# Order of the products inside one place of an attention and expert kernel: long products of both tiles first, then the diagonal blocks of both

## The chip, the cores and the metric

The kernel runs on one core of one Trainium2 chip. The metric is the device time of one execution in microseconds (us), the median over several runs. In the profile PE is TensorE with its matmuls, PEld are TensorE's weight loads (a matmul is a load of its stationary operand and the product itself), DVE is VectorE, ACT is ScalarE, POOL is GpSimd, and SP and ACT issue DMAs. L661 is line 661 of the kernel.

## The reference, cut to what matters

Sixteen sequences of 512 tokens with 256 channels pass through one transformer layer: attention with 16 heads of 16 channels, rotary positions and an ALiBi bias, a layer norm, a mixture of 8 experts with the best 2 chosen (and a shared expert), and a second layer norm.

```python
q = q * cos + _rotate_half(q) * sin
k = k * cos + _rotate_half(k) * sin
attn = jnp.einsum('bhqd,bhkd->bhqk', q, k) * SCALE
diff = jnp.where(pos[None, :] - pos[:, None] > 0, 0.0, pos[None, :] - pos[:, None])
attn = attn + (diff[None, :, :] * slopes[:, None, None] * MAX_BIAS)[None]
w = jax.nn.softmax(attn, axis=-1)
out = jnp.einsum('bhqk,bhkd->bhqd', w, v)
...
x = _layernorm(x + attention(x))
x = _layernorm(x + silu(x @ sW1 + sb1) @ sW2 + sb2 + two experts of eight, weighted)
```

## The kernel before, in words

All work is cut into numbered places s. A place from 0 to 511 (NC is 512) computes one 256 by 512 piece of the scores of one head, as two tiles k = 0 and 1 of 128 queries by 512 keys. It does this twice, for two purposes, with 14 places (LAG) between them:

- The score part of place s (tile pS, two banks, one for each k) gives the scores with queries on the partitions. DVE takes the negated maximum of every row (`row_max`, L965), one `tensor_reduce` for each k. The maxima go back through DRAM into two rows of the query operand.
- The turned part of place d = s - 14 (tile pT, two banks) gives the transposed scores, with the maxima subtracted. ACT takes their exponentials (`exps`, L1417), one activation for each k, into ee.

Each bank gets one long product (`score_rows` L661, `turned_rows` L682; 512 columns, 62 or 64 rows of the array) and on top of it two short diagonal blocks of 64 columns in bf16 (`score_block` L667, `turned_block` L688), which carry the part of the bias inside the diagonal. The second block of a bank raises s_s or s_t, and DVE or ACT starts on that bank. Score part and turned part of one place use opposite halves of the array's rows (slice 64 * hh), so their products can run side by side.

pS and pT have one bank for each k and no second set. So the long product of tile k of place s waits until the reduction of tile k of place s - 1 has ended (s_max), and the turned one until the exponential of tile k of place d - 1 has (s_exp).

The function `pair(s)` writes out the order on TensorE. APART holds all 32 residues, so in every place the order is: long products of k = 0 (score, turned), blocks of k = 0, long products of k = 1, blocks of k = 1. In the first 14 places, which have no turned part, and the last 14, which have no score part, `beside` (L696) puts a product on the unused bank, whose result nobody reads.

Behind `pair(s)` TensorE has in the same place whatever falls due by tables of fixed offsets: the products of the exponentials with the values (`weighted_values`, L710), the projections of queries, keys and values (L734, L743), the output projection (L756), and the transposes and expert products (L829, L837, L845, L847). DVE and ACT go through the same places with their own parts of these jobs, each queue in program order; `row_max(s)` and `exps(s - LAG)` come first in their place.

Of the kernel before, what the change touches and what calls it, by code (L numbers as in the profile page):

```python
# [6 lines left out]
ALU = mybir.AluOpType  # L7
ACT = mybir.ActivationFunctionType
# [3 lines left out]
F32R = mybir.dt.float32r  # L12
U32 = mybir.dt.uint32
AX = mybir.AxisListType.X
# [4 lines left out]
NC = NB * 32  # L19
LAG = 14  # L20


APART = tuple(range(32))
PV = (1, 3)
EPS = 1e-5
NBOUND = 7
# [173 lines left out]
def _build(nc, ctx, A, out):  # L200
    def sb(name, shape, dt=F32):
        return ctx.enter_context(nc.sbuf_tensor(name, shape, dt))

    def ps(name, shape, dt=F32):
        return ctx.enter_context(nc.psum_tensor(name, shape, dt))
# [4 lines left out]
    def sem(name):  # L210
        return ctx.enter_context(nc.semaphore(name))
# [4 lines left out]
    qa = [sb(f"qa{i}", [128, 2, T]) for i in range(4)]  # L216
    ka = [sb(f"ka{i}", [128, 2, T]) for i in range(4)]
    ee = sb("ee", [128, 2, 7, T])
# [24 lines left out]
    tri = sb("tri", [128, 4, 128], BF16)  # L243
    mAB = sb("mAB", [128, 2, 8, 64], BF16)
    sl = sb("sl", [128, H])
    slb = sb("slb", [128, H], BF16)
    slp = sb("slp", [128, 7, H])
    slc = sb("slc", [128, 1])
    negm = sb("negm", [128, 2, 4, 4])
# [53 lines left out]
    pS = ps("pS", [128, 2, T])  # L303
    pT = ps("pT", [128, 2, T])
# [53 lines left out]
    s_s, s_max, s_t, s_exp, s_pv, s_ev = (sem(n) for n in ("s_s", "s_max", "s_t", "s_exp", "s_pv", "s_ev"))  # L358
# [279 lines left out]
    def _(e):  # L638
# [6 lines left out]
        def score_wait(s):  # L645
            if s == 0:
                warm(WARM[3])
                e.wait_ge(p_w, 16)
                warm(WARM[4])
            g = s // 8  # L650
            e.wait_ge(qk_in[g % 4], group_in(g))
            if s == 0:
                e.wait_ge(l_tri, 32)
                e.wait_ge(s_slope, 4)

        def score_rows(s, k):
            if s > 0:
                e.wait_ge(s_max, 2 * (s - 1) + k + 1)
            g, i, t, hh = s // 8, (s // 4) % 2, 2 * (s % 2) + k, (s // 2) % 2
            r = slice(64 * hh, 64 * hh + 62)  # L660
            e.matmul(pS[:, k, :], qa[g % 4][r, i, t * 128:t * 128 + 128].bitcast(F32R),  # L661
                     ka[g % 4][r, i, :].bitcast(F32R), start=True, stop=False)

        def score_block(s, k, a):
            i, t, hh = (s // 4) % 8, 2 * (s % 2) + k, (s // 2) % 2
            r, c0 = slice(64 * hh, 64 * hh + 64), t * 128 + 64 * a
            last = e.matmul(pS[:, k, c0:c0 + 64], tri[r, a, :], mAB[r, 1, i, :], start=False, stop=(a == 1))  # L667
            if a == 1:
                last.then_inc(s_s, 1)

        def turned_wait(d):
            g = d // 8
            e.wait_ge(m_in[g % 2], 32 * (g // 2 + 1))

        def turned_rows(d, k):
            if d > 0:
                e.wait_ge(s_exp, 2 * (d - 1) + k + 1)
            g, kt, i, hh = d // 8, 2 * (d // 4 % 2) + k, d % 2, d // 2 % 2  # L680
            r = slice(64 * hh, 64 * hh + 64)
            e.matmul(pT[:, k, :], ka[g % 4][r, i, kt * 128:kt * 128 + 128].bitcast(F32R),  # L682
                     qa[g % 4][r, i, :].bitcast(F32R), start=True, stop=False)

        def turned_block(d, k, a):
            kt, i, hh = 2 * (d // 4 % 2) + k, 2 * (d // 8 % 4) + d % 2, d // 2 % 2
            r, c0 = slice(64 * hh, 64 * hh + 64), kt * 128 + 64 * a
            last = e.matmul(pT[:, k, c0:c0 + 64], tri[r, 2 + a, :], mAB[r, 0, i, :], start=False, stop=(a == 1))  # L688
            if a == 1:
                last.then_inc(s_t, 1)  # L690

        def beside(p, s, k):

            g, i, t, hh = s // 8, (s // 4) % 2, 2 * (s % 2) + k, (s // 2) % 2
            r = slice(64 * hh, 64 * hh + 62)
            e.matmul(p[:, k, :], qa[g % 4][r, i, t * 128:t * 128 + 128].bitcast(F32R),  # L696
                     ka[g % 4][r, i, :].bitcast(F32R), start=True, stop=True)
# [178 lines left out]
        def pair(s):  # L876
            d = s - LAG
            if 0 <= s < NC:
                score_wait(s)
            if 0 <= d < NC:  # L880
                turned_wait(d)
            apart = s % 32 in APART
            for k in range(2):
                if 0 <= s < NC:
                    score_rows(s, k)
                if 0 <= d < NC:
                    turned_rows(d, k)
                if 0 <= s < LAG:
                    beside(pT, s ^ 2, k)
                if NC <= s < NC + LAG:  # L890
                    if s == NC:
                        e.wait_ge(s_max, 2 * NC)
                    beside(pS, (d & -4) + (0, 2)[d // 2 % 2 == 0], k)
                for kk in ((k,) if apart else (0, 1) if k == 1 else ()):
                    for a in range(2):
                        if 0 <= s < NC:
                            score_block(s, kk, a)
                        if 0 <= d < NC:
                            turned_block(d, kk, a)

        e.wait_ge(s_zb0, 1)
        warm(WARM[0])
        for s in range(FIRST, LAST):
            pair(s)
            for k in range(2):
                w, r = divmod(s - LAG - PV[k], 4)
# [41 lines left out]
    def _(e):  # L948
# [10 lines left out]

        def row_max(s):  # L960
            g, j, t = s // 8, (s // 2) % 4, 2 * (s % 2)
            if s % 32 in APART:
                for k in range(2):
                    e.wait_ge(s_s, 2 * s + k + 1)
                    e.tensor_reduce(negm[:, g % 2, j, t + k:t + k + 1], pS[:, k, :], AX, ALU.max, negate=True).then_inc(s_max, 1)  # L965
            else:
                e.wait_ge(s_s, 2 * s + 2)
                e.tensor_reduce(negm[:, g % 2, j, t:t + 2], pS[:, :, :], AX, ALU.max, negate=True).then_inc(s_max, 2)

        def m_split(g):  # L970
            i = g % 2
# [311 lines left out]
        for x in (*rb2, sb2):  # L1283
            last = e.tensor_copy(x[:, :].bitcast(F32R), zb[:, 0:C])
# [46 lines left out]
        for s in range(FIRST, LAST):  # L1331
            if 0 <= s < NC:
                row_max(s)
# [72 lines left out]
    def _(e):  # L1406
        def exps(d):
            w, j = d // 4, 2 * (d % 2) + d // 2 % 2
            if d > 6:
                e.wait_ge(s_pv, (d - 7) // 4 + 1)  # L1410
            if d == 0:
                e.wait_ge(b_w, 64)
            h = (d // 8 % 4) * 4 + j
            if (d + LAG) % 32 in APART:
                for k in range(2):
                    e.wait_ge(s_t, 2 * d + k + 1)
                    e.activation(ee[:, k, d % 7, :], pT[:, k, :], ACT.Exp, scale=slp[:, 6, h:h + 1]).then_inc(s_exp, 1)  # L1417
            else:
                e.wait_ge(s_t, 2 * d + 2)
                e.activation(ee[:, :, d % 7, :], pT[:, :, :], ACT.Exp, scale=slp[:, 6, h:h + 1]).then_inc(s_exp, 2)  # L1420

        def evacuate(g):
            e.wait_ge(s_pv, 2 * g + 2)
# [114 lines left out]
        for s in range(FIRST, LAST):  # L1538
            if 0 <= s - LAG < NC:
                exps(s - LAG)  # L1540
# [248 lines left out]
```

## Time and profile before

| | |
|---|---|
| three runs | 1585.77, 1590.22, 1663.03 us; median 1590.22 us |
| the profiled execution | 1581.27 us, of which the span from first to last instruction is 1579.5 us |
| mean granted clock of TensorE in it | 0.967 |
| busy: PE, DVE, ACT, POOL | 1443.7, 1143.5, 1022.9, 717.3 us |
| chain that ended last, by engine | PE 65%, DVE 16%, issue 5%, DMA 4%, ACT 3% |

Busy time of an engine is the time covered by its instructions. The ends of matmuls are modelled and they are pipelined, so the distance between the starts of successive instructions tells more than their lengths. A row of the timeline gives start, length, engine, line, operation and the count of merged instructions; the part in brackets is the idle time before it on its engine and what ended it. DVE and ACT instructions in a merged row of two overlap a little.

### The profile page before, as it was taken

The page shows a single profiled execution, that of the slowest core. Times are in us where ns is not written, and L with a number is a line of the kernel's source. Part 1 is how long each engine was busy: PE and PEld are TensorE (multiplying, and loading weights), DVE is VectorE, ACT ScalarE, POOL GpSimd, SP SyncE. Part 2 cuts the span into 40 slices and gives each one's busy share as a digit, 9 for nine tenths or more (in the row PEclk, how much of TensorE's full clock was granted, in tenths as well). Part 3 has the DMA queues.
Part 4 walks back from the last instruction along what each step waited for, and adds up shares of the span by engine and source line. Part 5 has one row for each costly group of instructions (what it writes and reads, how often), then busy time and mean ns, then how long its engine had stood idle before and what let it go on. Part 6 is the DMA issues. An engine that isn't in the chain of part 4 may idle for free.

```text
span 1579.5 us, 33115 instructions
## 1 busy us (share of the span) xinstructions
PE 1443.7 (91%) x11166; PEld 790.4 (50%) x11166; DVE 1143.5 (72%) x2632; ACT 1022.9 (65%) x1742; POOL 717.3 (45%) x654
## 2 busy tenths in 40 slices
PE   7888999999999989999999999999998898888877
PEld 4433444444444445555555544455555555545545
DVE  7675877787787897667666788778875577644677
ACT  1365766676767667767777767676675576666434
POOL 2333363635546453643535353636475443354451
PEclk8799999999999999999999999999999999989899
DMA  7436343334343334555545443445576576368552
GB/s 203 137 95 190 102 123 111 117 111 127 121 124 119 115 109 154 160 162 174 173 154 173 129 144 110 131 159 169 182 226 216 158 221 215 112 209 262 194 155 84
DMA packets 176389, 242.00 MB, mean 153 GB/s; under 512 B 58023, under 2 KB 94974, under 8 KB 176222
## 3 DMA queue, kind: packets, MB, share of 16 engines
q1 hardware_dynamic: 145786, 181.18, 37.7%
q0 software_dynamic: 10752, 29.37, 5.7%
q10 hardware_dynamic: 19684, 29.33, 5.3%
q8 instruction: 91, 1.49, 0.4%
q14 instruction: 76, 0.62, 0.1%
HBM read 152.53 MB, written 91.44 MB: 154 GB/s over the span
## 4 chain that ended last, share of the span: by engine, by line
PE 65%; DVE 16%; SPq 5%; issue 5%; DMA 4%; ACT 3%; another core or an unknown queue 2%; POOL 0%; ACTq 0%; DVEq 0%; POOLq 0%
PE pS L661 18%; PE pV L710 12%; PE pG L734 7%; DVE negm L965 5%; PE pG L756 3%; PE pS L667 3%; PE pG L743 3%; PE pG L837 3%; PE pG L845 3%; PE pT L688 2%; PE pT L682 2%; PE pG L829 2%; PE pG L818 2%; ACT ee L1417 1%
## 5 line engine op out<-in xcount | busy, mean ns | idle before, releaser
L965 DVE TENSOR_REDUCE negm<-pS 128x1 f32<-128x512 f32 x1024 | 658.9, 683 | 281.6 <-PE pS L667 236.8
L1417 ACT ACTIVATE ee<-pT,slp 128x512 f32<-128x512 f32 x1024 | 650.7, 684 | 236.2 <-PE pT L688 208.7
L661 PE MATMUL pS<-ka,qa 62*128 62x512 f32 x1024 | 471.1, 495 | 59.2 <-DVE negm L965 47.9
L682 PE MATMUL pT<-qa,ka 64*128 64x512 f32 x1024 | 471.6, 494 | 8.7 <-ACT ee L1417 7.0
L661 PEld LDWEIGHTS pS<-ka,qa 62*128 62x128 f32 x1024 | 193.0, 188 | 316.8 <-issue 290.8
L710 PE MATMUL pV<-ee,vv 128*32 128x512 f32 (+1 forms) x2048 | 284.1, 627 | 0.0
L667 PE MATMUL pS<-mAB,tri 64*128 64x64 bf16 x2048 | 239.2, 198 | 0.0
L688 PE MATMUL pT<-mAB,tri 64*128 64x64 bf16 x2048 | 236.8, 196 | 0.0
L1604 POOL TENSOR_TENSOR raw<-raw,rope 128x512 f32<-128x512 f32 x61 | 77.9, 1276 | 302.6 <-DVE sh L1005 300.5
L682 PEld LDWEIGHTS pT<-qa,ka 64*128 64x128 f32 x1024 | 191.8, 187 | 20.5 <-issue 11.6
L667 PEld LDWEIGHTS pS<-mAB,tri 64*128 64x128 bf16 x2048 | 117.1, 97 | 132.8 <-issue 101.2
L1624 POOL TENSOR_TENSOR rs<-ve,minus 128x4 f32<-128x4 f32 x32 | 34.2, 1068 | 280.9 <-DVE ve L1053 280.7
L734 PE MATMUL pG<-xT,wqkv 128*128 128x512 f32 x256 | 144.6, 649 | 5.3 <-DVE wqkv L1320 2.9
L1639 POOL DMA_INDIRECT d_x<-x,pos x112 | 113.2, 1010 | 56.6 <-DVE pos L1100 32.3
L688 PEld LDWEIGHTS pT<-mAB,tri 64*128 64x128 bf16 x2048 | 115.9, 96 | 25.5 <-issue 21.2
L1668 POOL TENSOR_TENSOR pvs<-pvs 128x512 f32<-128x512 f32 x31 | 39.4, 1272 | 132.4 <-DVE pvs L990 132.3
L837 PE MATMUL pG<-xgT,wb 128*128 128x256 f32 x308 | 85.5, 402 | 13.9 <-ACT xgT L1505 6.3
L845 PE MATMUL pG<-wb,zbb 128*128 128x256 f32 x308 | 93.4, 396 | 2.1 <-ACT xgT L1505 1.4
L1661 POOL DMA_INDIRECT gg<-d_y,posy x72 | 71.1, 987 | 33.7 <-issue 20.8
L1521 ACT ACTIVATE yb<-pG 128x512 f32<-128x512 f32 x77 | 45.9, 597 | 61.7 <-PE pG L847 47.9
L1616 POOL TENSOR_TENSOR parts<-raw,parts 128x512 fp32r<-128x512 f32 x61 | 77.8, 1275 | 5.0
L1609 POOL TENSOR_TENSOR raw<-raw,sh 128x512 f32<-128x512 f32 x61 | 77.9, 1277 | 4.8
(203 smaller groups left out, 2179.8 us busy)
## 6 DMA issues: line engine op xcount, KB each, us to landing
d_part<-parts SPq DMA_DIRECT2D x63, 512.0 KB, 2.8
qa<-d_part SPq DMA_DIRECT2D x378, 64.0 KB
wb<-in_wb SPq DMA_DIRECT2D x77, 256.5 KB
xg<-d_x SPq DMA_DIRECT2D x77, 256.0 KB
d_y<-yb ACTq DMA_DIRECT2D x77, 256.0 KB
ka<-d_part SPq DMA_DIRECT2D x128, 128.0 KB
xT<-in_xT SPq DMA_DIRECT2D x16, 512.0 KB
ka<-d_part SPq DMA_DIRECT2D x128, 64.0 KB
```

The lines of the kernel that those rows point to most:

```text
L661: e.matmul(pS[:, k, :], qa[g % 4][r, i, t * 128:t * 128 + 128].bitcast(F32R), ka[g % 4][r, i, :].bitcast(F32R), start=True, stop=False)
L667: last = e.matmul(pS[:, k, c0:c0 + 64], tri[r, a, :], mAB[r, 1, i, :], start=False, stop=(a == 1))
L682: e.matmul(pT[:, k, :], ka[g % 4][r, i, kt * 128:kt * 128 + 128].bitcast(F32R), qa[g % 4][r, i, :].bitcast(F32R), start=True, stop=False)
L688: last = e.matmul(pT[:, k, c0:c0 + 64], tri[r, 2 + a, :], mAB[r, 0, i, :], start=False, stop=(a == 1))
L710: last = e.matmul(pV[32 * hh:32 * hh + m, :], vv[b % 2][:, 17 * kt + r0:17 * kt + r0 + m, h], ee[:, k, (4 * w + 2 * (hh % 2) + hh // 2) % ...
L734: last = e.matmul(pG[bk("qk", i, b)][:, :], wqkv[:, c, col:col + 128], xT[b % 2][:, c, :], start=(c == 0), stop=(c == 1))
L837: last = e.matmul(p[:, 0:ROWS], wb[q % 4][:, c * 128:c * 128 + 128], xgT[q % 2][:, c, :], start=(c == 0), stop=(c == 1))
L845: e.matmul(p[:, k * C:(k + 1) * C], zbb[q % 2][:, k * 128:k * 128 + 128], wb[q % 4][:, 256:512], start=True, stop=False)
L965: e.tensor_reduce(negm[:, g % 2, j, t + k:t + k + 1], pS[:, k, :], AX, ALU.max, negate=True).then_inc(s_max, 1)
L1417: e.activation(ee[:, k, d % 7, :], pT[:, k, :], ACT.Exp, scale=slp[:, 6, h:h + 1]).then_inc(s_exp, 1)
L1604: e.tensor_tensor(raw[:, :], raw[:, :], rope[:, 0, :], ALU.mult).then_inc(s_rope, 1)
L1639: e.indirect_dma_start(d_x[g % 2], bass.IndirectOffsetOnAxis(pos[:, b % 2, n, t:t + 1], 0), x1[b % 2][:, t, :], None).then_inc(rows_w, 16)
```

## The change

Inside `pair(s)` the four groups are reordered: long products of k = 0, long products of k = 1, then the blocks of k = 0, then the blocks of k = 1. The waits are split off from the long products (`score_free`, `turned_free`), so that both waits of a k stand ahead of both long products of that k; `beside` now stands ahead of the long products of its k. The semaphores are the same: the second block of each bank raises s_s or s_t, and DVE and ACT still work bank by bank. The branches for places not in APART, which no place took, are gone.

```diff
+        def score_free(s, k):
             if s > 0:
                 e.wait_ge(s_max, 2 * (s - 1) + k + 1)
+
+        def score_rows(s, k):
             g, i, t, hh = s // 8, (s // 4) % 2, 2 * (s % 2) + k, (s // 2) % 2
...
+        def turned_free(d, k):
             if d > 0:
                 e.wait_ge(s_exp, 2 * (d - 1) + k + 1)
...
-            apart = s % 32 in APART
+            def blocks(k):
+                for a in range(2):
+                    if 0 <= s < NC:
+                        score_block(s, k, a)
+                    if 0 <= d < NC:
+                        turned_block(d, k, a)
+
             for k in range(2):
                 if 0 <= s < NC:
-                    score_rows(s, k)
+                    score_free(s, k)
                 if 0 <= d < NC:
-                    turned_rows(d, k)
+                    turned_free(d, k)
                 if 0 <= s < LAG:
                     beside(pT, s ^ 2, k)
...
-                for kk in ((k,) if apart else (0, 1) if k == 1 else ()):
-                    for a in range(2):
-                        if 0 <= s < NC:
-                            score_block(s, kk, a)
-                        if 0 <= d < NC:
-                            turned_block(d, kk, a)
+                if 0 <= s < NC:
+                    score_rows(s, k)
+                if 0 <= d < NC:
+                    turned_rows(d, k)
+            for k in range(2):
+                blocks(k)
```

The matmuls of the long products and blocks also get `skip_group_check=True`, which adds no instruction.

## Rows read from the trace of the kernel before

**Rows 1.** The page, part 1: busy time, share of the span, instructions.
```profile
PE 1443.7 (91%) x11166; PEld 790.4 (50%) x11166; DVE 1143.5 (72%) x2632; ACT 1022.9 (65%) x1742; POOL 717.3 (45%) x654
```

**Rows 2.** Busy time by stretch of time, 200 to 1200 us in five stretches.
```profile
core 0: us, PE busy (x) PEld busy (x) DVE busy (x) ACT busy (x) POOL busy (x), PEclk, DMA share, GB/s
...
sum 1000.00, PE 952.54 PEld 499.81 DVE 759.47 ACT 702.52 POOL 493.85; mean PE 190.51 PEld 99.96 DVE 151.89 ACT 140.50 POOL 98.77
```

**Rows 3.** Costliest groups: busy us, mean ns of one | idle before, releaser.
```profile
L965 DVE TENSOR_REDUCE negm<-pS 128x1 f32<-128x512 f32 x1024 | 658.9, 683 | 281.6 <-PE pS L667 236.8
...
L661 PE MATMUL pS<-ka,qa 62*128 62x512 f32 x1024 | 471.1, 495 | 59.2 <-DVE negm L965 47.9
```

**Rows 4.** Waits of PE: us in total, times, longest.
```profile
PE pS L661 <- DVE negm L965: 47.9, 66, 3.0
...
PE pT L682 <- ACT ee L1417: 7.0, 14, 1.2
```

**Rows 5.** Timeline of PEld, one place without a wait on DVE or ACT.
```profile
706.53 0.18 PEld L661 LDWEIGHTS pS<-ka,qa 62*128 62x128 f32 x1 [0.17 <-issue]
...
706.88 0.10 PEld L667 LDWEIGHTS pS<-mAB,tri 64*128 64x128 bf16 x1 [0.16 <-issue]
...
706.93 0.19 PEld L661 LDWEIGHTS pS<-ka,qa 62*128 62x128 f32 x1
...
707.27 0.09 PEld L667 LDWEIGHTS pS<-mAB,tri 64*128 64x128 bf16 x1 [0.16 <-issue]
...
707.44 0.30 PEld L734 LDWEIGHTS pG<-xT,wqkv 128*128 128x128 f32 x2
```

**Rows 6.** Timeline of DVE and ACT, the same place.
```profile
707.15 1.29 DVE L965 TENSOR_REDUCE negm<-pS 128x1 f32<-128x512 f32 x2 [2.13 <-PE pS L667]
707.25 1.26 ACT L1417 ACTIVATE ee<-pT,slp 128x512 f32<-128x512 f32 x2
```

**Rows 7.** Timeline of PEld and PE, a place of the first 14.
```profile
50.71 0.18 PEld L661 LDWEIGHTS pS<-ka,qa 62*128 62x128 f32 x1 [0.76 <-issue]
50.71 0.29 PEld L696 LDWEIGHTS pT<-ka,qa 62*128 62x128 f32 x2
...
50.71 0.50 PE L696 MATMUL pT<-ka,qa 62*128 62x512 f32 x1
...
51.05 0.39 PE L696 MATMUL pT<-ka,qa 62*128 62x512 f32 x1
```

**Rows 8.** Timeline of DVE and PEld, a place that waits on DVE.
```profile
107.09 1.29 DVE L965 TENSOR_REDUCE negm<-pS 128x1 f32<-128x512 f32 x2 [0.17 <-PE pS L667]
108.30 0.24 DVE L986 RECIPROCAL scr<-sc 128x16 f32<-128x16 f32 x1
108.52 1.29 DVE L965 TENSOR_REDUCE negm<-pS 128x1 f32<-128x512 f32 x2
...
108.43 0.18 PEld L661 LDWEIGHTS pS<-ka,qa 62*128 62x128 f32 x1
```

**Rows 9.** Timeline of ACT and PEld, a short place and its successor.
```profile
1099.09 1.26 ACT L1417 ACTIVATE ee<-pT,slp 128x512 f32<-128x512 f32 x2 [0.68 <-PE pT L688]
...
1098.38 0.18 PEld L661 LDWEIGHTS pS<-ka,qa 62*128 62x128 f32 x1 [0.76 <-issue]
...
1100.28 0.18 PEld L661 LDWEIGHTS pS<-ka,qa 62*128 62x128 f32 x1 [0.83 <-issue]
...
1100.67 0.19 PEld L661 LDWEIGHTS pS<-ka,qa 62*128 62x128 f32 x1
```

**Rows 10.** Timeline of PEld: ends of the two counted sets of intervals.
```profile
30.39 0.18 PEld L661 LDWEIGHTS pS<-ka,qa 62*128 62x128 f32 x1
...
52.65 0.18 PEld L661 LDWEIGHTS pS<-ka,qa 62*128 62x128 f32 x1 [0.33 <-issue]
...
1358.00 0.18 PEld L661 LDWEIGHTS pS<-ka,qa 62*128 62x128 f32 x1 [0.17 <-issue]
...
1376.51 0.18 PEld L661 LDWEIGHTS pS<-ka,qa 62*128 62x128 f32 x1
```

More of the change, by code:

```diff
@@ L20 @@
 LAG = 14
-APART = tuple(range(32))
 PV = (1, 3)
@@ L654, in score_wait @@
                 e.wait_ge(s_slope, 4)
-        def score_rows(s, k):
+        def score_free(s, k):
             if s > 0:
                 e.wait_ge(s_max, 2 * (s - 1) + k + 1)
+        def score_rows(s, k):
             g, i, t, hh = s // 8, (s // 4) % 2, 2 * (s % 2) + k, (s // 2) % 2
@@ L661, in score_rows @@
             e.matmul(pS[:, k, :], qa[g % 4][r, i, t * 128:t * 128 + 128].bitcast(F32R),
-                     ka[g % 4][r, i, :].bitcast(F32R), start=True, stop=False)
+                     ka[g % 4][r, i, :].bitcast(F32R), start=True, stop=False, skip_group_check=True)
         def score_block(s, k, a):
@@ L666, in score_block @@
             r, c0 = slice(64 * hh, 64 * hh + 64), t * 128 + 64 * a
-            last = e.matmul(pS[:, k, c0:c0 + 64], tri[r, a, :], mAB[r, 1, i, :], start=False, stop=(a == 1))
+            last = e.matmul(pS[:, k, c0:c0 + 64], tri[r, a, :], mAB[r, 1, i, :], start=False, stop=(a == 1), skip_group_check=True)
             if a == 1:
@@ L675, in turned_wait, with turned_rows @@
             e.wait_ge(m_in[g % 2], 32 * (g // 2 + 1))
-        def turned_rows(d, k):
+        def turned_free(d, k):
             if d > 0:
                 e.wait_ge(s_exp, 2 * (d - 1) + k + 1)
+        def turned_rows(d, k):
             g, kt, i, hh = d // 8, 2 * (d // 4 % 2) + k, d % 2, d // 2 % 2
@@ L682, in turned_rows @@
             e.matmul(pT[:, k, :], ka[g % 4][r, i, kt * 128:kt * 128 + 128].bitcast(F32R),
-                     qa[g % 4][r, i, :].bitcast(F32R), start=True, stop=False)
+                     qa[g % 4][r, i, :].bitcast(F32R), start=True, stop=False, skip_group_check=True)
         def turned_block(d, k, a):
@@ L687, in turned_block @@
             r, c0 = slice(64 * hh, 64 * hh + 64), kt * 128 + 64 * a
-            last = e.matmul(pT[:, k, c0:c0 + 64], tri[r, 2 + a, :], mAB[r, 0, i, :], start=False, stop=(a == 1))
+            last = e.matmul(pT[:, k, c0:c0 + 64], tri[r, 2 + a, :], mAB[r, 0, i, :], start=False, stop=(a == 1), skip_group_check=True)
             if a == 1:
@@ L961, in row_max @@
             g, j, t = s // 8, (s // 2) % 4, 2 * (s % 2)
[L962 to L968, printed above, removed]
+            for k in range(2):
+                e.wait_ge(s_s, 2 * s + k + 1)
+                e.tensor_reduce(negm[:, g % 2, j, t + k:t + k + 1], pS[:, k, :], AX, ALU.max, negate=True).then_inc(s_max, 1)
         def m_split(g):
@@ L1413, in exps @@
             h = (d // 8 % 4) * 4 + j
[L1414 to L1420, printed above, removed]
+            for k in range(2):
+                e.wait_ge(s_t, 2 * d + k + 1)
+                e.activation(ee[:, k, d % 7, :], pT[:, k, :], ACT.Exp, scale=slp[:, 6, h:h + 1]).then_inc(s_exp, 1)
         def evacuate(g):
```

## The prediction

> **What bounds the kernel now.** I read the page's busy times first: PE is busy 91% of the span, DVE 72%, ACT 65% [rows 1]. Then the stretches: in the middle 1000 us PE is busy 95%, DVE 76%, ACT 70% [rows 2]. So PE sets the pace as a mean, but not by much: DVE and ACT have 1.3 us of work on the two banks in every place and other work besides. Then the groups: of DVE's idle time before the reductions, 237 of 282 us ends with a block of PE [rows 3]; DVE mostly waits for PE, and the other way round PE waits before L661 for DVE 66 times, 47.9 us in all, and for ACT before L682 7.0 us [rows 4]. The reader is to see two loops there: PE through a place, and the hand-over of a bank from PE to DVE or ACT and back. The change shortens the first and lengthens the second, so both must be measured.
>
> I went to the timeline for that. A place without a wait [rows 5] runs: long loads of k = 0 at 706.53, block loads at 706.88 (0.35 later), long loads of k = 1 at 706.93 (0.05 later), blocks at 707.27, next job at 707.44 (0.12 behind the last block). `pair` holds TensorE for 0.90 us. DVE starts at 707.15, 0.61 us behind the place's first load; ACT at 707.25, 0.71 behind it [rows 6]. The two reductions end 1.29 us after they start, so at 1.90 behind the first load.
>
> **Part 1: the order on TensorE.** Nothing is added or removed in number; 8 blocks, 4 long products remain. What is new is that a long load of k = 1 follows a long product of k = 0 in the same half of the array. Two cases in the trace tell what a load does there. A bf16 block load behind a long product starts only 0.34 to 0.35 us behind that product's load, so after the product has streamed [rows 5]. A 32-bit long load behind a 32-bit long product starts under it: in the first 14 places the half used by `beside` has no blocks between its two products, and the two L696 loads together take 0.29 us where one takes 0.18; the second starts 0.11 us behind the first, and its product starts at 51.05, 0.34 behind the first [rows 7]. So in the new order: long loads of k = 0 at 0, of k = 1 at 0.11, second long products at 0.34, block loads at 0.34 + 0.22 = 0.56 (they came 0.22 to 0.23 behind the start of a long product's streaming before: 0.35 less the 0.11 of the load), then the four blocks of k = 0 in 0.05, those of k = 1 in 0.06, and 0.12 to the next job: 0.79 us, or 0.78 with the unrounded starts. Against 0.90 that saves 0.11 to 0.12 us a place where PE runs without waiting. I take 0.12; from below the bound is 0 (no load is hidden), from above 0.18, one whole long load.
>
> The Trainium skill has a rule that speaks against this: "TensorE: Matmul & The Clock Gate", section "Part 3: Packing small matmuls", says that a weight load overlaps a running product only when it goes to another group of rows. By it the saving would be 0, and the case becomes rival C below. The trace disagrees in rows 7, where both L696 loads go to the same rows.
>
> Two waits now stand ahead of one load, where each load had one; one of them becomes an instruction of its own. The nearest rows are a load that waited: it came 0.05 behind the end of the reduction that it waited for, everything of the hand-back included [rows 8]. Where the semaphores are already up, this runs ahead of the array under the products queued there, and costs nothing; a second 0.05 in every place, 26 us, is its bound from above. I take 0, since in most places they are up. That the score's product waits also for the exponential, in the same place where the turned one waited, moves it by a few hundredths of a us. `beside` ahead of its product touches 28 places and costs nothing.
>
> **Part 2: the hand-over of the banks.** The blocks of k = 0 are now queued behind the long products of k = 1, and these behind the waits for the last reduction and last exponential of the place before. Without a wait DVE starts at 0.56 + 0.27 = 0.83 behind the place's first load instead of 0.61 (0.27 is 707.15 less 706.88), so all reductions and exponentials end 0.21 later than now. And the long load of k = 1 wants to start at 0.11 instead of 0.39, that is 0.28 earlier. So the margin between the end of the last reduction (or exponential) and the long load of k = 1 of the next place shrinks by 0.49; 0.12 of this costs nothing, because the load may come that much late under the running product. A place whose margin now is m therefore loses 0.37 - m where m is below 0.37.
>
> In a stretch where DVE never rests, this is seen at its worst [rows 8]: reductions end at 108.38, the long load of k = 1 comes 0.05 later, and DVE finds bank 0 ready and starts again at 108.52. In the new order the blocks of bank 0 stand behind that load, and DVE starts at 108.43 + 0.61 = 109.04, 0.5 us later. The least interval of a place becomes 0.59 + 0.68 + 0.05 + 0.71 = 2.03 us by way of ACT (start to start of its two exponentials, the second, the hand-back, the hand-over); now intervals of 1.42 us occur. A typical short place [rows 9]: loads at 1098.38 and 1100.28, 1.90 apart, exponentials end at 1100.35, the long load of k = 1 is at 1100.67: m = 0.32, so it loses 0.05.
>
> **The sum.** I took all 511 intervals between the first long loads of successive places. In 356 of them PE waits for nothing (the second begins at 52.65, the last ends at 1358.00): 356 x 0.12 = 43 us gained. In 241 (the first is the one whose k = 1 load stands at 30.39, the last at 1376.51) the margin is below 0.37, and the shortages add up to 52 us [rows 10]. The median margin is 0.42. The two add up to +9 us. I counted it in a second way, by length: 157 intervals are shorter than 2.0 (134 with a mean of 1.93, 23 with a mean of 1.52) and grow to 2.02: 134 x 0.09 + 23 x 0.50 = +24 us; 55 between 2.0 and 2.15 shrink by 0.06: -3; of 299 longer ones 201 have no wait and shrink by 0.12: -24; 23 of these 201 have margins below 0.37, +10. That gives +7. I take +8 us. Other work of DVE and ACT between two places is cover for the longer hand-over; if it were gone the 299 longer intervals would still be longer than 2.03, so they need none.
>
> The profiled execution took 1581.3 us, of which 1579.5 are the span; it would become 1589. The median of the runs lies 8.9 us above the profiled execution, so on the median's scale the forecast is 1590 + 8 = 1598 us, +0.5%. A measurement of this kernel tells about 2%, 32 us, from no change.
>
> **The rivals.**
>
> A (slower): the hand-over becomes the pace. The place is the long load of k = 1, which waits for the last exponential of the place before. It decides if the margins count in full: nothing of the lost 0.49 is hidden, because the late load also puts the block loads late. The 293 intervals below 0.49 fall short by 84 us; less the 43 gained that is +41: 1631 us. For it: the median margin of 0.42 is below 0.49, and DVE, busy 76% in the middle [rows 2], has little left to catch up with. Against it: rows 7 show the slack of 0.12 under the product.
>
> B (faster): the shortages are absorbed and the waiting places gain too. 29 of the 52 us of shortage lie in intervals where PE waits already for something, often a DMA; if these cost nothing, 23 remain, and if the 155 waiting intervals gain 0.12 as well (19 us), the sum is -43 - 19 + 23 = -39: 1551 us. For it: many of the shortest intervals catch up behind a longer one. Against it: most waits of L661 are for DVE itself [rows 4], which gets later.
>
> C (slower): the second long load isn't hidden. The blocks of k = 0 come at 0.34 + 0.34 = 0.68, `pair` stays at 0.91, reductions end 0.34 later and the load of k = 1 wants to come 0.05 earlier: shortages below 0.39 add up to 57 us, and no gain: 1647 us. For it: block loads are never seen under a long product. Against it: rows 7.
>
> **How the numbers follow.** Forecast 0.66, A 0.15, B 0.09, C 0.05; 0.05 for anything else, on both sides. The range goes from half of B's gain, -20 (gain 43, shortages only 23 outside waiting intervals), to A's +41: 1570 to 1632. The forecast's own range is 1580 to 1618. Faster by over 2% (below 1558) needs B, 0.07. Slower by over 2% (above 1622) is A, C and a little of the rest: 0.20. Within 2%: 0.73.
>
> **What would show it right or wrong.** In a place without a wait the second L661 load stands 0.11 behind the first, block loads at 0.56, the next job at 0.79; if the second load is at 0.34, it is C. The first reduction starts 0.83 behind the place's first load. Intervals below 1.95 are gone. Waits of PE before L661 for DVE, and before L682 for ACT, grow from 48 and 7 us together to over 80. PE's busy time falls by some tens of us, while the idle time grows by a little more. It is wrong if the intervals above 2.15 don't shrink, or if the short ones don't grow.

## The result and the profile after

The changed kernel takes 1634.6 us (median of four runs, 1627.4 to 1644.9) against 1588.0 for the kernel before on the same chip: ratio 1.0319, with an interval of 1.0279 to 1.0359. It is 3.2% slower. One slow run of the kernel before, 1663.0 us, stands in its median and not in the ratio, which is why the ratio isn't quite the quotient of the two medians. The forecast was 1598, 8 us above the kernel before, with a range from 1570 to 1632. The sign was right; the change cost 47 us by the medians, and the measured time lies 3 us above the range. On a second chip, where the kernel before takes 1545 us, the ratio was 1.0176 (1.0140 to 1.0212).

The page of the changed kernel, parts 1 and 4, answers to [rows 1]:

```profile
PE 1461.0 (89%) x11166; PEld 780.6 (48%) x11166; DVE 1144.6 (70%) x2632; ACT 1016.5 (62%) x1742; POOL 719.7 (44%) x654
...
PE 62%; DVE 11%; SPq 7%; ACT 7%; issue 5%; DMA 5%; another core or an unknown queue 3%; POOL 1%; ACTq 0%; POOLq 0%; DVEq 0%
```

DVE and ACT do the same work in the same time, in a span that is 60 us longer. PE's busy time rose by 17 us, with the same instructions. Its groups, from part 5, answer to [rows 3]:

```profile
L971 DVE TENSOR_REDUCE negm<-pS 128x1 f32<-128x512 f32 x1024 | 658.5, 684 | 353.9 <-PE pS L668 304.0
...
L1419 ACT ACTIVATE ee<-pT,slp 128x512 f32<-128x512 f32 x1024 | 649.6, 684 | 344.9 <-PE pT L689 306.6
...
L662 PE MATMUL pS<-ka,qa 62*128 62x512 f32 x1024 | 444.8, 479 | 92.4 <-ACT ee L1419 41.2
```

A reduction is as long as it was (684 against 683 ns), but DVE waits 304 us for block products, where it waited 237. PE's idle time before the score's long product went from 59 to 92 us, and the largest part of it, 41 us, now ends with an exponential. These two numbers show only a part of the delay, because the modelled ends of the products reach into the time in which TensorE waits. PEld shows more of it, in the idle time ahead of the score's long loads; before and after:

```profile
L661 PEld LDWEIGHTS pS<-ka,qa 62*128 62x128 f32 x1024 | 193.0, 188 | 316.8 <-issue 290.8
```

```profile
L662 PEld LDWEIGHTS pS<-ka,qa 62*128 62x128 f32 x1024 | 179.0, 191 | 421.3 <-issue 329.8
```

It is 104 us more. Part of this has only moved: ahead of the score's block loads (L667, now L668) the idle time fell from 133 to 96 us. The waits of PE, against [rows 4]:

```profile
PE pS L662 <- ACT ee L1419: 41.2, 62, 2.3
PE pS L662 <- DVE negm L971: 24.5, 24, 2.4
```

Before, ACT held PE for 7.0 us and DVE for 47.9. The sum went from 55 to 66 us, and the releaser changed: for the larger part it is ACT now.

A place in which nothing holds TensorE, weight loads alone, against [rows 5]:

```profile
734.43 0.18 PEld L662 LDWEIGHTS pS<-ka,qa 62*128 62x128 f32 x1 [0.23 <-issue]
...
734.54 0.19 PEld L662 LDWEIGHTS pS<-ka,qa 62*128 62x128 f32 x1
...
735.00 0.09 PEld L668 LDWEIGHTS pS<-mAB,tri 64*128 64x128 bf16 x1 [0.28 <-issue]
...
735.23 0.22 PEld L711 LDWEIGHTS pV<-ee,vv 128*32 128x32 f32 x8
```

The second long load comes 0.11 us behind the first, the blocks 0.57, the next job 0.80 (0.91 before). DVE's row of the same place, against [rows 6], starts 0.85 behind the first load (0.62 before):

```profile
735.28 1.29 DVE L971 TENSOR_REDUCE negm<-pS 128x1 f32<-128x512 f32 x2 [1.20 <-PE pS L668]
```

That is the place as it was forecast. But most places don't look like this. Two that follow each other, first the weight loads, against [rows 8]:

```profile
469.94 0.18 PEld L662 LDWEIGHTS pS<-ka,qa 62*128 62x128 f32 x1 [0.83 <-issue]
...
470.45 0.18 PEld L662 LDWEIGHTS pS<-ka,qa 62*128 62x128 f32 x1 [0.32 <-DVE negm L971]
...
470.78 0.11 PEld L668 LDWEIGHTS pS<-mAB,tri 64*128 64x128 bf16 x2
...
472.09 0.18 PEld L662 LDWEIGHTS pS<-ka,qa 62*128 62x128 f32 x1 [0.76 <-issue]
...
472.54 0.18 PEld L662 LDWEIGHTS pS<-ka,qa 62*128 62x128 f32 x1 [0.26 <-DVE negm L971]
```

and ACT's two pairs of exponentials in them:

```profile
469.06 1.27 ACT L1419 ACTIVATE ee<-pT,slp 128x512 f32<-128x512 f32 x2
471.16 1.26 ACT L1419 ACTIVATE ee<-pT,slp 128x512 f32<-128x512 f32 x2 [0.83 <-PE pT L689]
```

The second long load stands 0.51 and 0.45 behind the first, not 0.11. The row names DVE as its releaser, but the pair of exponentials ended last, at 469.06 + 1.27 = 470.33, and the load follows 0.12 behind. The next exponential starts 0.71 behind that load. So from one pair of exponentials to the next it is 471.16 - 469.06 = 2.10 us, of which ACT stands idle for 0.83. Of 497 places with both parts and such a place before them, the score's load of k = 1 follows within 0.12 us behind an exponential in 245, and behind a reduction in 57. In the kernel before, where each load had its own wait, the turned load followed an exponential in 87 places and the score's load a reduction in 92.

### The profile page after: what moved, and what is told of

The parts are those of the page before. It is cut to its first block, busy times and chain, and to the rows that moved or that the text cites. A ratio compares the mean times of both kernels' runs of the same rounds, so it can differ in the third digit from the quotient of the medians.

```text
span 1639.2 us, 34110 instructions
## 1 busy us (share of the span) xinstructions
PE 1461.0 (89%) x11166; PEld 780.6 (48%) x11166; DVE 1144.6 (70%) x2632; ACT 1016.5 (62%) x1742; POOL 719.7 (44%) x654
## 4 chain that ended last, share of the span: by engine, by line
PE 62%; DVE 11%; SPq 7%; ACT 7%; issue 5%; DMA 5%; another core or an unknown queue 3%; POOL 1%; ACTq 0%; POOLq 0%; DVEq 0%
PE pS L662 19%; PE pV L711 12%; PE pG L735 6%; ACT ee L1419 4%; PE pG L744 3%; DVE negm L971 3%; PE pG L757 3%; PE pG L838 2%; PE pS L668 2%; PE pT L689 2%; PE pG L846 2%; PE pG L819 2%; PE pG L806 1%; PE pG L830 1%
## 5 line engine op out<-in xcount | busy, mean ns | idle before, releaser
L662 PE MATMUL pS<-ka,qa 62*128 62x512 f32 x1024 | 444.8, 479 | 92.4 <-ACT ee L1419 41.2
L683 PE MATMUL pT<-qa,ka 64*128 64x512 f32 x1024 | 451.5, 486 | 0.0
L662 PEld LDWEIGHTS pS<-ka,qa 62*128 62x128 f32 x1024 | 179.0, 191 | 421.3 <-issue 329.8
L711 PE MATMUL pV<-ee,vv 128*32 128x512 f32 (+1 forms) x2048 | 295.6, 651 | 0.0
L683 PEld LDWEIGHTS pT<-qa,ka 64*128 64x128 f32 x1024 | 177.6, 190 | 0.0
L668 PE MATMUL pS<-mAB,tri 64*128 64x64 bf16 x2048 | 152.8, 196 | 0.0
L689 PE MATMUL pT<-mAB,tri 64*128 64x64 bf16 x2048 | 151.2, 195 | 0.0
L668 PEld LDWEIGHTS pS<-mAB,tri 64*128 64x128 bf16 x2048 | 90.9, 98 | 95.7 <-issue 64.7
L689 PEld LDWEIGHTS pT<-mAB,tri 64*128 64x128 bf16 x2048 | 89.6, 97 | 11.4 <-issue 11.0
L1605 POOL TENSOR_TENSOR sh<-sh,rope 128x512 f32<-128x512 f32 x61 | 78.1, 1281 | 0.0
```

The costliest lines, as they stand in the source:

```text
L711: last = e.matmul(pV[32 * hh:32 * hh + m, :], vv[b % 2][:, 17 * kt + r0:17 * kt + r0 + m, h], ee[:, k, (4 * w + 2 * (hh % 2) + hh // 2) % ...
```

## The experiments

In the diffs, `free(k)` stands for both waits of a k, `rows(k)` for its long products, `blocks(k)` for its four blocks. Every ratio is to the kernel before on the same chip. Five chips took part; the kernel before takes 1588, 1602, 1544, 1545 and 1545 us on them, so times are compared on one chip, or as ratios.

**e1: the old order with all four waits at the head of the place.** The products are those of before, and only the waits move.

```diff
-for k in range(2): free(k); rows(k); blocks(k)
+for k in range(2): free(k)
+for k in range(2): rows(k); blocks(k)
```

> The order of the products is that of the kernel before; only the waits move: all four of a place (reduction and exponential, k = 0 and 1) stand ahead of its first long product. Theory 1 (hand-over: tile 0 of a place can't be handed on until the last reduction and exponential of the place before have ended, while TensorE itself gets faster by 0.1 us a place): the same long loop as in the changed kernel, about 2.1 us at least for a place, without TensorE's gain. So slower than the changed kernel's 1635 us, by up to 0.1 x 250 = 25 us: 1635 to 1660 us, and no interval of a place below 2.0 us. Theory 2 (the extra wait instruction costs 0.06 us where it is on the path, little else): about 0.06 x 250 = 15 us over before, 1605 us. Theory 3 (the products' new order itself is slow on TensorE, or lowers its clock): no change from before, 1590 us.

Measured: 1708.4 against 1601.7, ratio 1.0676 (1.0629 to 1.0723). The waits of PE:

```profile
PE pS L662 <- ACT ee L1425: 81.3, 108, 7.5
PE pS L662 <- DVE negm L977: 47.6, 47, 2.8
```

Apart from the first two places, which have no turned part, no interval is below 2.11 us; before, a quarter was below 1.96. A late first long load alone, with no product moved, costs 107 us. So the hand-over of the banks is a pace that this kernel runs close to, and more of the waiting ends with ACT. The cost is more than was expected: 6.8%, where 1635 to 1660 us would have been 3% to 4.5% over the kernel before, and twice what the changed kernel loses. TensorE also stood at the lower of its two clock levels for 210 us in this trace (105 in the kernel before, on the first chip), so the 107 us are not the hand-over's pace alone.

**e2: the changed order, with each wait at its own long product again.**

```diff
 for k in range(2):
-    free(k); rows(k)
+    score_free(s, k); score_rows(s, k)
+    turned_free(d, k); turned_rows(d, k)
```

> The changed kernel's order of products, but each wait back ahead of its own product (the score's product waits for the reduction only, the turned one for the exponential only, and no load has two waits ahead of it). Theory 1 (hand-over): nearly the changed kernel, 1620 to 1630 us; the load of the turned product comes 0.05 us behind the exponential instead of 0.11, in about half of the places, so 10 to 15 us of the 47 go. Theory 2 (extra wait): most of it goes, 1600 us or less. Theory 3 (order on TensorE): no change from 1635 us.

Measured: 1633.8 against 1601.7, ratio 1.0224 (1.0174 to 1.0274). ACT's row and the weight loads of one place:

```profile
423.24 1.27 ACT L1417 ACTIVATE ee<-pT,slp 128x512 f32<-128x512 f32 x2 [1.27 <-PE pT L689]
```

```profile
424.49 0.18 PEld L662 LDWEIGHTS pS<-ka,qa 62*128 62x128 f32 x1 [0.32 <-DVE negm L969]
424.56 0.18 PEld L683 LDWEIGHTS pT<-qa,ka 64*128 64x128 f32 x1
```

The exponentials end at 424.51, and the turned load follows 0.05 behind; the score's load no longer waits for them. In the changed kernel it was 0.12 at 470.45, since the wait for ACT there is an instruction of its own (34110 instructions against 33115). Over all places of this kind it is 0.05 here and 0.11 there. What this is worth in time lies between the changed kernel's 1.018 and 1.032, both of other chips, and can't be told from them; most of the loss stays without it.

**e8: the old order, with both waits of a k ahead of its long products.**

```diff
 for k in range(2):
-    score_free(s, k); score_rows(s, k)
-    turned_free(d, k); turned_rows(d, k)
+    free(k); rows(k)
     blocks(k)
```

> The old order of products, but both waits of a tile (reduction and exponential) ahead of both its long products, as the changed kernel has them; this is the price of the extra wait instruction alone. About 100 places are held by the exponential in the trace of before, 0.06 us each: 6 us slower by theory 1, within 10 us. By theory 2 (the extra wait carries the loss) 30 us or more slower.

Measured: 1549.0 against 1543.8, ratio 1.0033 (1.0008 to 1.0057): 5 us, as expected. In the old order, where ACT seldom holds the load, the extra wait costs a third of a per cent.

**e3 and e4: the old order and the changed one, with reductions and exponentials over half of the columns.** Both leave out the other half of the row maxima and of the exponentials, and the products with the values read the first half twice. Product counts and shapes on TensorE stay.

```diff
-tensor_reduce(negm[...], pS[:, k, :], ...)
+tensor_reduce(negm[...], pS[:, k, 256:512], ...)
-activation(ee[:, k, d % 7, :], pT[:, k, :], ...)
+activation(ee[:, k, d % 7, 0:256], pT[:, k, 0:256], ...)
```

> Leaves out half of what DVE and ACT do with each bank: the reduction reads columns 256 to 511 only, the exponential makes columns 0 to 255 only, and the product with the values reads these twice, so that TensorE's work stays. The order of products is that of the kernel before. Each reduction should take about 0.42 us instead of 0.68, each exponential 0.45. All theories: somewhat faster than before, 1500 to 1560 us, bound by TensorE and the other waits.

> The changed kernel with the same half of reductions and exponentials left out. Theory 1 (hand-over): the least interval of a place falls from 2.1 to about 1.6 us, below TensorE's own 1.8 us in the shortest places, so the loop stops to bind and TensorE's gain of 0.1 us a place shows: 25 to 50 us faster than the kernel before with the same half left out. Theory 3 (the order is slow on TensorE): still some 45 us slower than that one. Theory 2 (extra wait only): near it, within 15 us.

Measured on one chip: 1563.0 in the old order, ratio 0.9772 (0.9714 to 0.9830), and 1544.2 in the changed one, ratio 0.9667 (0.9615 to 0.9719). The stretch of the places, first e3, then e4:

```profile
28.00:1353.00 1325.00, 1249.15 (x10348) 660.33 (x10346) 762.94 (x2209) 709.71 (x1544) 621.45 (x551) 0.98 0.50 151
```

```profile
27.00:1335.00 1308.00, 1201.37 (x10350) 631.01 (x10350) 746.18 (x2209) 709.50 (x1545) 626.06 (x552) 0.98 0.50 153
```

With short reductions and exponentials the change turns over: it is 19 us, 1.2%, faster, and PE's busy time falls by 48 us. This is less than the 25 to 50 us that were expected. The saving of Part 1 is real, and much of what eats it hangs on the length of the reduction and the exponential. Not all of it does: counted as in the table further down, `pair` is 28 us shorter in e4 than in e3 at full clock, and the rest of the intervals is still 21 us longer.

**c3 and c4: the changed kernel with only the exponentials halved, and with only the reductions halved.** c3 leaves out the exponentials of the second half of the columns; c4 takes the row maxima over columns 256 to 511 alone.

> The changed kernel with half of each exponential left out (columns 0 to 255 only are made, and read twice by the product with the values), the reductions whole. Theory 1: ACT's loop (start to start 0.59, last one 0.68, hand-back 0.11, hand-over 0.72: 2.10 us) falls to about 1.6, and DVE's (0.61 + 0.68 + 0.05 + 0.62 = 1.96 us, or 2.03 with the second wait) holds the place: 10 to 25 us faster than the changed kernel, and still slower than before by 1% or more.

> The changed kernel with half of each reduction left out (columns 256 to 511 only are read), the exponentials whole. Theory 1: ACT's loop of 2.10 us still holds the short places, so little is won there, 0 to 15 us against the changed kernel; what is won comes from places where DVE is late by its other work. If more comes from this one than from c3, DVE's queue and not the exponential's hand-over was the cause.

Measured: c3 1548.7, ratio 1.0031 (1.0011 to 1.0051); c4 1546.7, ratio 1.0004 (0.9984 to 1.0025). On this chip the unedited changed kernel takes 1575.0, ratio 1.0176 (c2 below), so c3 wins 26 us and c4 28. Both are more than was expected (10 to 25, and 0 to 15 us), and they can't be told apart, so neither engine is singled out by this. The traces show that the two loops lie close together: the load of k = 1 stands within 0.12 us behind an exponential in 266 places of c4 (237 in c2), but in c3, with short exponentials, it stands behind a reduction in 306 (64 in c2).

**d3: the kernel before with only the reductions halved**, the partner of c4; its row maxima too are taken over columns 256 to 511 alone.

> The kernel before with the reductions over columns 256 to 511 only, to tell what of d1 is the order and what the shorter reduction. TensorE holds the places by its 0.90 us and its other work, and DVE is held mostly by it: 10 to 20 us faster than before. If d1 gains no more than this one does, the order adds nothing once DVE is light.

Measured: 1503.2 against 1545.0, ratio 0.9723 (0.9686 to 0.9761): 42 us faster, where 10 to 20 were expected. The kernel before wins 2.8% by shorter reductions, the changed one 1.7% (1.0176 to 1.0004). So with DVE relieved the change costs more, 2.9% (1.0004 over 0.9723, on two chips with the same time for the kernel before), not less. The loss doesn't need the full length of the reductions. That ACT's hand-over carries it then is argued from this and from the 266 places of c4, not shown: the kernel before with only the exponentials halved, the partner of c3, was not run.

**e6 and e7: the changed order in some places only.** e6 has it in ten of each 32 places (9, 11 to 15, 24, 27, 30, 31), those with much other work behind them; e7 in the other 22. Both keep the old order in the first and the last 14 places.

```diff
+wide = s % 32 in (9, 11, 12, 13, 14, 15, 24, 27, 30, 31)   # e7: not in
 for k in range(2):
     rows(k)
-    blocks(k)
+    if not wide: blocks(k)
+if wide:
+    for k in range(2): blocks(k)
```

> The changed kernel's order in ten of every 32 places only (s mod 32 = 9, 11 to 15, 24, 27, 30, 31), those in which the trace of before shows a margin above 0.2 us in the place and above 0.33 us in the next one, in three cases of four or more; the old order in the other places and in the first and last 14. Theory 1 (margins decide): 155 places x 0.1 = 16 us gained, nothing lost: 1% faster than before, at worst the same. If the cost of the change is spread over all places (theory 2 or 3): a third of it, 10 to 15 us slower.

> The other way round: the changed kernel's order in the other 22 of every 32 places, the old order in those ten and in the first and last 14. Theory 1: all of the loss and none of the sure gain: 50 + 16 us slower than before, 4% (a little less for the 28 places left out). Theory 2 or 3: two thirds of the changed kernel's loss, 2%.

Measured: e6 1545.0, ratio 1.0012 (0.9992 to 1.0033): no gain, a miss, for -1% was expected. e7 1567.9, ratio 1.0146 (1.0109 to 1.0182): slower as expected, but by 1.5% and not 4%. A loss of 1.8% (c2) spread evenly over all places would put 0.5% on the ten, an estimate from that ratio, and e6's interval ends at 0.33%. So the loss sits in the 22 places, and the long places, which were to bring the gain, bring none.

**c1 and c2: the kernels before and after once more, with traces of one chip.** No edit.

> The kernel before, unchanged, for a trace on the same chip as the next three. All theories: the time of the kernel before on this chip; the trace gives its margins and the stretches at the lower clock for a comparison with c2_after_again without a change of chip.

> The changed kernel, unchanged, beside the kernel before on this chip. If the loss is the hand-over of tile 0 (theory 1) it is there on every chip, 2.5% to 3.5% slower. If a good part of it was particular to the chip of the first comparison (its DMA times), the ratio is 1.5% to 2.5%. Where the slower chips wait longer, TensorE's clock falls more often too.

Measured: 1544.5 (one run) and 1575.0, the latter with ratio 1.0176 (1.0140 to 1.0212). This is the second branch of the expectation for c2: a good part of the 3.2% belongs to the first chip. The waits of PE, in c1 and in c2:

```profile
PE pS L661 <- DVE negm L965: 40.8, 71, 2.5
```

```profile
PE pS L662 <- ACT ee L1419: 27.7, 49, 1.3
PE pS L662 <- DVE negm L971: 19.5, 22, 2.2
```

and the stretch of the places and what is behind it, in c1 and in c2:

```profile
27.00:1352.00 1325.00, 1255.68 (x10357) 665.29 (x10355) 1025.27 (x2210) 914.91 (x1546) 625.78 (x552) 0.98 0.50 151
1352.00:1545.00 193.00, 150.99 (x752) 103.28 (x752) 121.59 (x372) 101.04 (x189) 89.46 (x93) 0.93 0.59 187
```

```profile
27.00:1383.00 1356.00, 1264.12 (x10350) 656.60 (x10350) 1007.07 (x2209) 907.29 (x1544) 622.88 (x552) 0.97 0.48 148
1383.00:1580.00 197.00, 155.57 (x762) 103.90 (x755) 121.00 (x372) 101.72 (x189) 89.69 (x93) 0.91 0.58 184
```

The difference of the two, interval by interval (from one place's first long load to the next's), worked out from the starts in both traces. "Pair" is the time from a place's first long load to the first load behind its blocks; "this chip" is c2 less c1, "first chip" the changed kernel less the kernel before:

| part | this chip, us | first chip, us |
|---|---|---|
| pair: shorter by some 0.1 | -24 (212 places) | -26 (206) |
| pair: longer by over 0.05 | +37 (209) | +37 (194) |
| pair, all intervals at full clock | +12 | +10 |
| rest of the interval, at full clock | +12 | +28 |
| intervals at the lower clock in one of the two traces or in both | +9 | +19 |
| behind the 511 intervals | +5 | +3 |
| ahead of them | -1 | -1 |

But for rounding, the last five lines add up to the +36 and +60 us by which the spans differ.

The rest of the interval needs a closer look. Nearly all of its growth, 12 of 12 and 25 of 28 us, stands directly ahead of the next place's first long load, and no more than 3 us stand inside the other jobs. In 11 and 24 us of it, that load follows at once behind the exponential of k = 0 of the place before (within 0.15 us) or behind its reduction (within 0.24 us). So it is bank 0 that the load waits for there, and not bank 1. One such place, number 370, ACT and the first long load, before:

```profile
928.56 0.69 ACT L1417 ACTIVATE ee<-pT,slp 128x512 f32<-128x512 f32 x1 [0.24 <-issue]
```

```profile
929.27 0.18 PEld L661 LDWEIGHTS pS<-ka,qa 62*128 62x128 f32 x1 [0.65 <-issue]
```

and after:

```profile
977.82 1.27 ACT L1419 ACTIVATE ee<-pT,slp 128x512 f32<-128x512 f32 x2 [0.94 <-PE pT L689]
```

```profile
978.62 0.18 PEld L662 LDWEIGHTS pS<-ka,qa 62*128 62x128 f32 x1 [1.27 <-issue]
```

The first exponential of the pair ends 0.69 behind its start, at 978.51, and the load follows 0.11 behind. The load stood behind the exponential before as well, but the idle time ahead of it grew from 0.65 to 1.27 us, because the blocks of k = 0, and so the exponential, came later. A few such places carry most of it: on the first chip 16 of 452 intervals hold 19.5 of the 28 us.

**e5 and d2: the blocks of k = 0 first.** The blocks of bank 0 go ahead of its long product, the first of them clears the bank, and the long product raises the semaphore. It is meant to shorten TensorE's part and to leave the hand-over as early as it was. d2 is e5 again on another chip.

```diff
-for k in range(2): free(k); rows(k)
-for k in range(2): blocks(k)
+blocks(0)      # start=True on the first block, waits at the first use
+rows(0)        # raises s_s, s_t
+rows(1)
+blocks(1)
```

> A third order, with every wait ahead of its own product: blocks of k = 0 first (the first of them clears the bank), then the long products of k = 0, which now raise the semaphore of tile 0, then the long products of k = 1, then the blocks of k = 1. The long load of k = 1 still follows a long product of k = 0 and one change from 32-bit to bf16 loads a place is saved, so TensorE should need 0.79 us a place as in the changed kernel instead of 0.90; but tile 0 is handed on ahead of the wait for tile 1, as in the kernel before. Theory 1 (the cost of the change is the hand-over of tile 0): 0.1 us x 350 places gained and nothing lost, 20 to 45 us faster than before. Theory 3 (two long products in a row are slow on TensorE or lower its clock): slower than before by up to 45 us.

> e5 once more, unchanged, on whatever chip this is: 1% to 1.5% faster than before on every chip if the gain is TensorE's order and not a matter of one chip's DMA times.

Measured: 1528.6 against 1543.8, ratio 0.9882 (0.9844 to 0.9921); again 1527.4 against 1545.0, ratio 0.9878 (0.9843 to 0.9913). It is 15 and 18 us faster; 20 to 45 were expected of e5. Weight loads of a place without a wait, and DVE in it:

```profile
703.59 0.09 PEld L670 LDWEIGHTS pS<-mAB,tri 64*128 64x128 bf16 x1 [0.17 <-issue]
...
703.63 0.19 PEld L662 LDWEIGHTS pS<-ka,qa 62*128 62x128 f32 x1
...
703.74 0.19 PEld L662 LDWEIGHTS pS<-ka,qa 62*128 62x128 f32 x1
...
704.21 0.10 PEld L670 LDWEIGHTS pS<-mAB,tri 64*128 64x128 bf16 x1 [0.27 <-issue]
```

```profile
704.18 1.28 DVE L986 TENSOR_REDUCE negm<-pS 128x1 f32<-128x512 f32 x2
```

The reductions start 0.59 us behind the place's first load, where it was 0.62 before and 0.85 in the changed kernel, and the second long product still goes straight behind the first. In the median the pair holds TensorE for 0.79 us from its first block load (0.74 from its first long load), where it was 0.90 in the kernel before (c1) and 0.95 in the changed one (c2), waits in it counted, all at full clock. This version beats both kernels.

**d1: e5 with the reductions halved** (row maxima over columns 256 to 511 alone).

> The blocks-first order of e5 (tile 0 handed on ahead of the wait for tile 1) with the reductions over columns 256 to 511 only. Theory 1: DVE's loop is then much shorter than TensorE's own time in every place and only ACT's stays; the places where DVE was late by its other work gain too. 15 to 30 us faster than e5, 2% to 3% faster than before.

Measured: 1480.8, ratio 0.9599 (0.9564 to 0.9634), the fastest of all, and 47 us faster than d2 on the same chip, where 15 to 30 were expected. Beside d3's 0.9723 the order with the blocks first is again worth 1.3%.

## Why the prediction was wrong

**What bounds the kernel: right.** Two loops, PE's part shortened and the hand-over lengthened. e3 with e4, and e1, show each: 1.2% won where the reductions and exponentials are short, 6.8% lost where only the hand-over is later.

**Part 1, the order on TensorE: right in its shape.** Second long load 0.11 behind the first, blocks 0.57 for 0.56, next job 0.80 for 0.79, first reduction 0.85 for 0.83. (The prediction's "0.35 less the 0.11" is 0.24, not 0.22 to 0.23; the 0.57 has that.) The rule of the Trainium skill ("TensorE: Matmul & The Clock Gate", "Part 3: Packing small matmuls"), weighed there against rows 7, would have put that load behind the product; in the row at 734.54 it starts 0.11 behind a load for the same rows of the array, so on this kernel the trace disagrees with it, and rival C is out.

**Part 2 and the sum: right as a net, wrong in what it left out.** The forecast was 52 of shortages less 43 of gain, +9. For the pair the traces show +12 and +10, which is close, but by luck: both halves were too large. The shortages came to 37, and "356 x 0.12 = 43 us gained" was counted in every place that had no wait before, yet only some 210 places became shorter, by 24 to 26 us. A place without a wait is no sign of slack: in 245 places the load of k = 1 now stands directly behind an exponential. The second count, by length, fails in the same way. The intervals above 2.15 were to shrink by 0.12 each where they had no wait. On the second chip the 257 of them at full clock together grew by 1.3 us: the pair gained 6 and the rest of the interval gave back 8. On the first chip 267 grew by 19. e6 says the same of ten places: nothing.

**The step that failed** is therefore "The two add up to +9 us", taken as the whole effect on the time. Three terms were set at nothing or were not in it:

- The margin of bank 0. "A place whose margin now is m therefore loses 0.37 - m" was counted at the long load of k = 1 alone. But every reduction and exponential of a place without a wait starts 0.2 us later, those of k = 0 too, and the next place's first long load waits for them. This is most of the +12 and +28 us outside the pair (11 and 24), as at 978.62. That other work of DVE and ACT is cover for the longer hand-over doesn't hold there. The jobs of PE between two places became longer by no more than 3 us.
- The clock. In the records TensorE stood at the lower level, 1.2 of 2.4 GHz, for 105 us before and 161 us after; on the second chip 89 and 121. It fell to it 17 and 33 times, on the second chip 15 and 23. The mean granted clock in the stretch of the places went from 0.98 to 0.96 (c1 to c2: 0.98 to 0.97). Intervals touched in either trace are +19 and +9 us. PE's busy time rose by 17 us where a fall was predicted, and this rise lies in these intervals; at full clock it stayed the same (0.4 us more). PE also stood idle for over 0.5 us more often, 74 and 110 times (66 and 85), but that this is what brought the clock down was not tried apart from the waits.
- The two waits ahead of one load, "I take 0, since in most places they are up". They are not up in 245 places, and there the extra wait makes the hand-back 0.11 us in place of 0.05: 245 x 0.06 = 15 us, an estimate from those rows that lies within the pair's +37. A first long load behind a reduction comes 0.23 behind it, in 70 places, where it came 0.12 behind in 68. e8's 5 us is the price of the extra wait where ACT seldom holds the load, and e2 shows that without it most of the loss stays.

**Rival A** named the mechanism, the hand-over as the pace, and 1631 us. The time fits the first chip, but its arithmetic doesn't: it put +41 into the pair, where +10 is. The least interval by way of ACT, 2.03 in Part 2, is 2.10 at 469.06; the difference is that extra wait. **Rival B**, that the shortages are absorbed, is excluded by the result and by e1 and e7. A further rival, that the new order is itself slow on TensorE or lowers its clock, is excluded by e4 and by e5, which keeps the two long loads together and is faster than both.

**What was to be seen.** Waits of PE for DVE and ACT together "over 80" us: they are 66, and the rest of the delay shows in PEld and in the table. "Intervals below 1.95 are gone": one in ten is still below it on both chips (48 and 50 of 511, from 113 and 110). That an interval can be short because the place before it began late is a likely reason, and not shown. "It is wrong if the intervals above 2.15 don't shrink": they don't. PE's busy time "falls by some tens of us": it does in e4 against e3, but not at full length of the engines.

Why the loss is 3.2% on one chip and 1.8% on another stays open. The kernel before also differs by 3% between them, and most of the difference is outside the pair (+28 against +12) and in the intervals at the lower clock (+19 against +9).

## What to carry to other kernels

When an order of products saves time on TensorE, ask when the first consumer can start and when its buffer is asked for again. Putting all long work first moves both ends of a single-buffered hand-over the wrong way; putting the short accumulating pieces first on the first bank got the saving with the hand-over nearly unchanged, and -1.2% in place of +1.8% on chips with the same time for the kernel before. Don't count a saving in every place that has no wait now. Take the margin of every buffer and every consumer, here of bank 0 as well as of bank 1, and look at the time spent at the lower clock in both traces.

## What the runs showed of the hardware

- Weight loads in fp32 for the same rows of the array start under the running product, 0.11 us behind the load before (734.43 and 734.54). A bf16 block load behind the same kind of product never comes sooner than 0.33 us behind that product's load, in all 512 places of the kernel before, the changed kernel and e5; the rows shown have 0.27 or 0.28 idle before it.
- A wait that is an instruction of its own, ahead of a load that is already held, puts 0.06 us on the hand-back from ACT (0.11 against 0.05, changed kernel and e2), and 0.11 on that from a reduction to a place's first long load (0.23 against 0.12, changed kernel and kernel before).
- One DVE instruction that takes 0.63 us elsewhere took 3.29 and 3.36 us in two of its 16 calls in the changed kernel, beside an addition of 128x1024 on POOL. It is not a matter of the change: in the first profile of the kernel before all 16 take 0.68 or less, but in c1, the same kernel, three took 3.07 to 3.08 beside that addition and seven others 1.13 or more, five of these 1.25 to 1.41. It was not tried apart. DVE's row, and POOL's:

```profile
472.43 3.36 DVE L1212 SCALAR_TENSOR_TENSOR hs<-th,zb 128x512 f32<-128x512 f32 x1
```

```profile
472.86 2.37 POOL L1673 TENSOR_TENSOR z<-z,pb 128x1024 f32<-128x1024 f32 x1
```
